# An adapter's weight generator one step later and in 64-row matmul pairs, and the last tiles turned on TensorE

## What is computed

```
scale = cond @ norm_w.T + 1.0
h = x * (scale[:, None, :] * rsqrt(mean(x * x) + EPS))
val, gate = split(h @ up_w.T)                  # 2 x 1024
y = act_quant(val * gelu(gate)) @ weight_quant(down_w).T + x

Wd_b = Wd + 0.1 * (cond @ Wdd.T + bdd)         # per sequence, 128 x 256
Wu_b = Wu + 0.1 * (cond @ Wdu.T + bdu)         # per sequence, 256 x 128
out = y + relu(y @ Wd_b.T + bd) @ Wu_b.T + bu
```

## Time and profile before

| | us |
|---|---|
| median of 3 runs (lowest, highest) | 486.35 (485.64, 487.13) |
| the profiled execution, its own time | 486.9 |
| its span, first to last instruction | 485.1 |
| TensorE busy with matmuls | 467.1 (96%) |
| VectorE, ScalarE, GpSimd busy | 384.2, 365.0, 267.8 |
| mean granted TensorE clock | 0.985 of full |

### The profile page before, as it was taken

How to read it: one execution, slowest core, us unless ns; L and a number is a source line. 1 busy time by engine, 2 the same in 40 slices (tenths; PEclk the granted TensorE clock), 3 DMA queues, 4 the chain that set the end, 5 groups by cost and what they waited for, 6 DMA issues and landing times.

```text
span 485.1 us, 9963 instructions
## 1 busy us (share of the span) xinstructions
PE 467.1 (96%) x3246; PEld 270.3 (56%) x3246; DVE 384.2 (79%) x776; ACT 365.0 (75%) x631; POOL 267.8 (55%) x683
## 2 busy tenths in 40 slices
PE   8859999999999999999999999999999999999955
PEld 7335656656655555555555555556555555555534
DVE  3796988989889878888888888887768777777783
ACT  4787999999996877687767767776777777777551
POOL 3397565775655556655654666565444444444443
PEclk9979999999999999999999999999999999999996
DMA  7937777889764565556545566564455454453443
GB/s 252 373 78 206 219 195 206 181 245 238 187 176 58 118 108 132 152 131 132 152 90 135 125 154 130 126 156 109 109 111 153 119 122 112 117 130 77 89 92 114
DMA packets 120547, 71.65 MB, mean 148 GB/s; under 512 B 104688, under 2 KB 105648, under 8 KB 118320
## 3 DMA queue, kind: packets, MB, share of 16 engines
q1 hardware_dynamic: 120336, 70.94, 59.2%
q10 hardware_dynamic: 160, 0.07, 0.1%
HBM read 37.44 MB, written 8.39 MB: 94 GB/s over the span
## 4 chain that ended last, share of the span: by engine, by line
PE 90%; POOL 4%; DVE 2%; issue 2%; ACT 1%; POOLq 0%; DVEq 0%; ACTq 0%
PE bank L838 65%; PE bank L848 11%; PE bank L862 5%; PE bank L886 4%; PE bank L876 4%; PE bank L809 1%; POOL wsplit L365 1%; POOL nwt L378 1%; POOL nwt L380 1%; POOL ad_lo L401 1%; DVE hid L650 0%; POOL nwt L376 0%; POOL nwt L383 0%; DVE xs_lo L629 0%; ACT gel L482 0%
## 5 line engine op out<-in xcount | busy, mean ns | idle before, releaser
L482 ACT ACTIVATE gel<-bank,rms 128x512 f32<-128x512 f32 x128 | 87.6, 685 | 94.2 <-PE bank L838 91.0
L650 DVE SCALAR_TENSOR_TENSOR hid<-bank,rms,gel 128x512 f32<-128x512 f32 x128 | 95.9, 749 | 76.3 <-ACT gel L482 75.1
L838 PE MATMUL bank<-up_hi,xs_hi 128*128 128x512 f16 x512 | 152.7, 380 | 1.7 <-DVE hid L650 1.5
L838 PE MATMUL bank<-up_hi,xs_lo 128*128 128x512 f16 x512 | 152.6, 380 | 0.0
L838 PE MATMUL bank<-up_lo,xs_hi 128*128 128x512 f16 x512 | 152.3, 379 | 0.1
L838 PEld LDWEIGHTS bank<-up_lo,xs_hi 128*128 128x128 f16 x512 | 49.9, 98 | 61.2 <-DVE up_lo L755 1.5
L838 PEld LDWEIGHTS bank<-up_hi,xs_lo 128*128 128x128 f16 x512 | 50.2, 98 | 60.7 <-issue 0.6
L658 DVE TENSOR_REDUCE amax<-hid 128x1 f32<-128x1024 f32 x63 | 76.9, 1220 | 2.2
L488 ACT ACTIVATE hid<-hid,amax 128x1024 f32<-128x1024 f32 x64 | 72.4, 1132 | 1.6 <-DVE amax L684 1.2
L365 POOL TENSOR_TENSOR wsplit<-stage,wsplit 128x288 f16<-128x288 f32 x64 | 53.0, 856 | 33.2 <-ACT wsplit L457 33.2
L848 PE MATMUL bank<-tern,qT 128*128 128x256 bf16 x512 | 66.6, 273 | 4.5 <-DMA qT<-qn 3.2
(11 more groups left out here) (90 smaller groups left out, 621.3 us busy)
## 6 DMA issues: line engine op xcount, KB each, us to landing
xT_s<-in_xT SPq DMA_DIRECT2D x32, 256.0 KB, 3.3
xn_s<-in_xn SPq DMA_DIRECT2D x32, 256.0 KB, 3.7
stage<-in_WddT SPq DMA_DIRECT2D x8, 1024.0 KB, 5.2
stage<-in_WduT SPq DMA_DIRECT2D x8, 1024.0 KB, 5.3
out<-out_s SPq DMA_DIRECT2D x31, 256.0 KB, 2.4
adapt<-in_up_wT SPq DMA_DIRECT2D x4, 512.0 KB, 7.4
x<-in_down_wT SPq DMA_DIRECT2D x1, 1024.0 KB, 10.6
qT<-qn SPq DMA_TRANSPOSE x64, 3.1
```

Of the source, the lines that this page charges most:

```text
L482: nc.scalar.activation(gel[:, c], u_gate[c][:], ACT.Gelu, scale=rms[:, t // TPB % XN_SLOTS, t % TPB:t % TPB + 1]).then_inc(gelu_done, 1)
L650: nc.vector.scalar_tensor_tensor(out=hid[:, t % 2, c * 512:(c + 1) * 512], in0=u_val[c][:], scalar=rms[:, t // TPB % XN_SLOTS, t % TPB:t % ...
L838: ins = nc.tensor.matmul(dst[:], a[:, t // TPB % 2, k, cols], w[:, c, k, v, :], start=(k == 0 and n == 0), stop=(k == KD - 1 and n == 2))
```

## The change

It has five parts.

1. **Generator matmuls.** `generate` uses the two halves of the array's rows separately: for each block of weights and pass, one matmul with partitions 0 to 63 and one with 64 to 127, each with 64 rows and 32 columns, into two different PSUM banks. A chunk has 96 matmuls instead of 48. `evacuate` takes bank by bank as before; the columns of `adapt` and `base` are ordered to fit, and the split of the adapter's weights reads them without a stride.
2. **Generator later.** `chunk` returns s - 2 - lag: every operation of the generator, its loads too, is one step later, and so is the start of the adapter in the early sequences (NGEN + 5). From b = 21 on `adapter_step` is 2b + 7 as before; the last three have no steps of their own any more.
3. **Start.** The first root mean square is computed by VectorE (`rsqrt_first`, 9 operations) in place of GpSimd; the next one's preparation, and gelu(0, 1), stand in step 0, ahead of the sum over down_w. `ternary_first` is behind `quant_scale(1)`, the other two passes behind `gate(2, 0)`. Loads of x 1 and 2 are issued earlier. GpSimd's sum of the bases is in step 1, its last operation in 4 parts.
4. **End.** The last `up(63, 1)` is two pieces of 256 columns each (24 matmuls of 256 columns, `up_last`), with gelu, gate and maximum by pieces. The last tile of quantized values and the x1 tiles 61, 62 and 63 are turned by TensorE with an identity (8 and 12 matmuls of 128 columns) and copied from PSUM by ScalarE and VectorE, where four transposing transfers stood. The last adapter weights are split in steps 60 to 62 (`adapter_splits`), the last sequence's buffers lie in `stage` and `wsplit`, and GpSimd takes the low parts of x1 for tiles 59 to 61.
5. **Order at the end.** Written out by hand; tile 63 goes ahead of tile 62.

The diff, cut to its core:

```diff
 def adapter_step(b):
 
-    if b >= B - 3:
-        return (NT, NT + 2, NT + 3)[b - B + 3]
-    return max(2 * b + 7, NGEN + 4 + (4 * b + 2) // 3)
+    return max(2 * b + 7, NGEN + 5 + (4 * b + 2) // 3)
...
-    return [s - 1 - lag] if 0 <= s - 1 - lag < NGEN else []
+    return [s - 2 - lag] if 0 <= s - 2 - lag < NGEN else []
...
+            load_x(1)
             sp.dma_start(raw_down, down_wT).then_inc(ld_down, 16)
-            load_x(1)
             load_chunk(0)
+            load_x(2)
             for i, (w, b) in enumerate(((WdT, bddT), (WuT, bduT))):
                 sp.dma_start(base[:, i, :], w).then_inc(ld_small, 16)
                 sp.dma_start(bias_raw[:, i, :], b).then_inc(ld_small, 16)
             sp.dma_start(bd_col[:], bd).then_inc(ld_small, 16)
             sp.dma_start(bu_row[:], bu.to_broadcast([P, D])).then_inc(ld_small, 16)
-            load_x(2)
             load_chunk(1)
-            for s in range(END):
...
-            for s in range(END):
+            for s in range(NT):
                 for b in sequences(s, -1):
-                    if b < LAST_B:
-                        relu(b)
-                    else:
-                        relu_last()
-                if s < NT:
-                    gelu(s, 0)
+                    relu(b)
+                gelu(s, 0)
                 if s == 0:
+                    scaled_high(1)
+                    squares(1)
+                    gelu(0, 1)
...
+            gelu_piece(1)
+            residual_high(LAST_T - 3)
+            relu(B - 4)
+            quantize(LAST_T)
+            quantized(LAST_T)
+            qT_evacuate()
+            residual_high(LAST_T - 2)
+            relu(B - 3)
+            residual_high(LAST_T - 1)
+            x61_evacuate()
+            x63_hi_evacuate()
+            relu(B - 2)
+            relu_last()
...
+            def rsqrt_first():
+                nh, y, tmp = nwt[:, 1], nwt[:, 2], nwt[:, 3]
+                for n in range(3):
+                    dve.wait_ge(guess_done, 2)
+                    after(dve, first_root, 3 * n)
+                    nc.vector.tensor_tensor(tmp, y, y, ALU.mult).then_inc(first_root, 1)
+                    dve.wait_ge(first_root, 3 * n + 1)
+                    nc.vector.tensor_tensor(tmp, tmp, nh, ALU.mult).then_inc(first_root, 1)
+                    dve.wait_ge(first_root, 3 * n + 2)
+                    if n < 2:
+                        nc.vector.scalar_tensor_tensor(out=y, in0=tmp, scalar=1.5, in1=y, op0=ALU.add, op1=ALU.mult
+                                                       ).then_inc(first_root, 1)
+                    else:
+                        nc.vector.scalar_tensor_tensor(out=rms[:, 0], in0=tmp, scalar=1.5, in1=y, op0=ALU.add, op1=ALU.mult
+                                                       ).then_inc(rms_done, 1)
+
             scaled_low(0)
             rsqrt_guess(0)
+            rsqrt_first()
...
+                if s == LAST_T:
+                    total(B - 5)
+                gate(s, 0)
+                if s == 0:
+                    scaled_low(1)
+                    rsqrt_guess(1)
                 if s == 2:
...
+            maximum_first()
+            gate_piece(0)
+            maximum_second()
+            gate_piece(1)
+            quantize_last()
+            residual(LAST_T - 2)
+            qT_evacuate()
+            residual(LAST_T - 1)
+            residual(LAST_T)
+            residual_high_last()
+            residual_low(LAST_T)
+            residual_low(LAST_T - 1)
+            x63_lo_evacuate()
+            x62_evacuate()
+            total(B - 4)
+            total(B - 3)
+            split_last()
+            total(B - 2)
+            total_last()
...
+                pe.wait_ge(qn_done, NT)
+                for n, pair in enumerate((0, 2, 1, 3)):
+                    if n == 1:
+                        pe.wait_ge(last_qn_done, 1)
+                    for j in range(2):
+                        f = 2 * pair + j
+                        ins = nc.tensor.matmul(qT_ps[pair][:, j * P:(j + 1) * P], qn[:, LAST_T % 2, f * P:(f + 1) * P],
+                                               ident_b[:], start=True, stop=True)
+                    ins.then_inc(q_turned, 1)
...
+            def x_transpose(t, dst, parts):
+                for c, part in enumerate(parts):
+                    for k in range(KD):
+                        at = (c * KD + k) * P
+                        ins = nc.tensor.matmul(dst[:, at:at + P], x1n[:, t % X1N_SLOTS, part, k * P:(k + 1) * P], ident[:],
+                                               start=True, stop=True)
+                ins.then_inc(x_turned, 1)
...
             def generate(q):
                 pe.wait_ge(w_lo_v, q + 1)
                 pe.wait_ge(w_lo_p, q + 1)
-                for n in range(2):
-                    after(pe, gen_done, 2 * q + n - 2)
-                    for m in range(BCH):
-                        dst = gen_ps[(2 * q + n) % 3][:].rearrange("p (h m b) -> p m h b", h=2, m=BCH)[:, m]
-                        cols = slice((n * BCH + m) * P, (n * BCH + m + 1) * P)
-                        passes = ((0, cdiag_hi), (0, cdiag_lo), (1, cdiag_hi))
-                        for k, (part, moving) in enumerate(passes):
-                            ins = nc.tensor.matmul(dst, wsplit[:, q % 2, part, cols], moving[:],
-                                                   start=(k == 0), stop=(k == len(passes) - 1))
-                    ins.then_inc(gen_full, 1)
+
+                after(pe, gen_done, 2 * q - 1)
+                for m in range(GCH):
+                    cols = slice(m * P, (m + 1) * P)
+                    passes = ((0, cdiag_hi), (0, cdiag_lo), (1, cdiag_hi))
+                    for k, (part, moving) in enumerate(passes):
+                        for h in range(2):
+                            rows = slice(h * C, (h + 1) * C)
+                            ins = nc.tensor.matmul(gen_ps[(2 * q + h) % 3][:, m * B:(m + 1) * B], wsplit[rows, q % 2, part, cols],
+                                                   moving[rows, h], start=(k == 0), stop=(k == len(passes) - 1))
+                            if m == GCH - 1 and k == len(passes) - 1:
+                                ins.then_inc(gen_full, 1)
...
+                if s < LAST_T:
+                    up(s, 1)
+                else:
+                    up_last(0)
+                    up_last(1)
...
+            down(LAST_T - 2)
+            middle(B - 3)
+            output(B - 4)
+            down(LAST_T - 1)
+            q_transpose()
+            down_last()
+            pe.wait_ge(late_lo_done, 3)
+            x_transpose(LAST_T - 2, x61_ps, (0, 1))
+
+            pe.wait_ge(last_x1_hi_done, 1)
+            x_transpose(LAST_T, x63_hi_ps, (0,))
+            pe.wait_ge(x1_lo_done, LAST_T - 3)
+            x_transpose(LAST_T, x63_lo_ps, (1,))
+            pe.wait_ge(x1_lo_done, LAST_T - 2)
+            x_transpose(LAST_T - 1, x62_ps, (0, 1))
+            output(B - 3)
+            middle(B - 2)
+            middle_last(1)
+            middle_last(0)
+            output(B - 2)
+            output_last()
```

424 lines of the change are left out of this document (279 added, 145 removed).

## The result

The changed kernel takes 481.29 us (median of 4 runs, 480.67 to 482.34) against 486.41 before; the ratio is 0.9897, with a 95% interval of 0.9871 to 0.9923. The gain is 5.1 us, where 14.7 (6.1 + 4.1 + 4.5) had been forecast. The profiled execution took 480.67, of which 478.9 is span: 6.2 less than the 485.1 of before. Medians and ratios here are of runs in the faster of the chip's two states, which leaves out two of the five runs of a_earlier (492.13 and 493.66 us).

The account below looks back on a forecast made before the run. TensorE was taken as the bound, busy 467.1 of 485.1 us. From the profiled 486.9, 6.1 (start), 4.1 (generator) and 4.5 (end) gave 472.2, median 472; its own range 468 to 478, 8-in-10 range 468 to 494.

Parts of the forecast that it names:

- The start: Up to the first chunk: earlier first gelu and split, generate(0) at 34.9; 6.1 us off, bounds 4 to 8.0.
- The generator's matmuls: Each chunk 0.96 us in place of 1.40, steps 7.2 in place of 7.49; 4.1 us off over 14 steps.
- 32 columns would be 15.8: Generator's matmul spacing in ns, from 2.5 ns plus the columns at 2.4 GHz, fitted to 512, 256 and 64 columns.
- Full overlap: Generator's pairs: both half-height matmuls run together, 0.76 us a chunk, 0.96 with mode changes; called the least sure term.
- the shared wait: Before each chunk, a wait w for GpSimd's split: step both 7.0 + w and 7.35 - w, so 7.2.
- rival (a): Generator gains nothing: pairs follow each other or the split's chain holds the step; 476 to 481 us, chance 0.28.
- TensorE's wait at even steps for x's low part: Middle, even steps: waiting for the low part, not only the high, is covered by most of a step.
- In the middle it costs nothing: Generator a step later: loads, splits and matmuls move together, each keeping its lead over the next; no cost.
- evacuate(q - 1, 0) ... counted as free: Whole chunk waits for this 1.05 us on VectorE behind residual, which ends some 0.2 before up(s, 1); no cost.
- The end: After the last up: pieces and TensorE turning, last add at 477.5 against 482.82; 4.5 us off, between 2.5 and 5.5.
- 0.4 + 0.4: End of the kernel, VectorE: us for the last two items in its row of adds and splits, to 472.0.
- The half clock: At the end, stretches at granted clock 0.50 double TensorE's share; 0.8 us taken off the 5.3 gain.

Follow-up runs that it names:

- a_earlier: Changed kernel with the generator's chunks and the adapters one step earlier, as in the kernel before: 483.21 us, ratio 0.9926.
- d_best2: Changed kernel with x's low part between evacuations, TensorE waiting for x's high part alone, GpSimd's last sums moved, base sum halved: 475.84 us, ratio 0.9766.
- e_low_first: Changed kernel with x's low part made on VectorE ahead of both evacuations of the generator's chunk: 487.63 us, ratio 1.0023.

## Why the prediction was wrong, point by point

- **The start, 6.1 us: right**, nearly in each time: first gelu 13.61 (13.85), up(1, 0) 15.94 (16.1), the new wait before up(3, 0) 1.39 (1.3), down(0) 30.57 (30.4), generate(0) 35.02 (34.9). Some of that is luck: the three passes over down_w took 2.29, 1.21 and 1.23, where 1.29, 1.3 and 1.72 had been counted, and the sum of the bases held GpSimd until 31.1, which I had not counted, while ScalarE was done 0.7 sooner than I had reckoned. With half of that sum moved away (d_best2) chunk 0 starts at 34.32. What I got wrong was whose the gain is: the root's move gave none of it, and the later generator, which I put at nothing, is indispensable to it.
- **The generator's matmuls, 4.1 us: wrong, and the largest miss.** The step that failed is "32 columns would be 15.8", a line laid through 512, 256 and 64 columns and drawn on to 32. Full overlap was right; the spacing is 25 ns a pair, 1.20 a chunk, where 15.8 and 0.76 had been taken, and the two changes of mode took 0.2 as supposed. 1.40 against 1.39: nothing. The trace had no spacing under 29.2, and the floor of the Trainium skill, which I had weighed and not taken, gave the 1.20. What then sets the step is TensorE at 7.45, so the shared wait that I reckoned never came into play. This was rival (a)'s result, by another way than (a) named.
- **"TensorE's wait at even steps for x's low part ... is covered by most of a step": wrong.** I looked at when x's high part is ready, not at what stands ahead of the low part in VectorE's program: 1.9 us of evacuation. It costs 0.2 at each of seven steps.
- **"In the middle it costs nothing": wrong by 1.3 us**, once, at steps 19 and 20. Lead over the next chunk is kept, but not the fall of odd and even: moved by one step, the last evacuations meet the low part. These two items and 0.1 in the last step with a chunk make 2.9; the kernel before lost 0.6 in its own fourth steps and its last one, so they explain 2.3 of the 2.5 lost in the middle. "evacuate(q - 1, 0) ... counted as free" was right, and e_low_first shows how narrowly.
- **The end, 4.5 us: right in its course, 1.9 too large.** To y of tile 63 all came as priced (residual at +6.2, forecast +6.0). Then "0.4 + 0.4" for the low parts was 0.85 each beside GpSimd, which I had listed apart without asking what runs at the same time; 1.7 in all with the splits. The half clock cost about 0.5 in the changed kernel's profile, of the 0.8 taken off. Behind the last add, 0.3 more passed until the end of the span than before. With GpSimd's sums moved away, 13.7 was reached, where 13.5 was forecast.
- **The range** of 468 to 494 held the result; the forecast's own, 468 to 478, did not. It came out at the upper edge of (a), 481.

## What to carry to other kernels

Splitting a matmul's rows into pairs helps only as far as the columns, at the clock of the moment, still take longer than the least distance between starts: here 64 columns take 29.2 ns at full clock and a pair can't start sooner than 25 ns after the last, so half the columns bought 4 ns for each of 48, and the changes of mode took them. When a stage is moved by one step, list for each engine what else falls in the new step, in each parity, and for each queue which item is due first; an operation that is "covered" is covered only if what stands ahead of it in its own queue is done. At an end that is one chain, ask which of VectorE's operations run beside GpSimd's, and move the ones that nobody waits for.
